# Sums on VectorE instead of GpSimd after the first weights are made, one sum of h made ahead, gates in fewer operations and asked for later

## The reference, cut to what matters

```python
def reference(x, itok_B_0_15, L0_cond_weights, L0_ffn_A, L0_ffn_B, L0_ffn_Wr):
    W = L0_cond_weights[itok_B_0_15]                 # (64, 64, 64), one 64x64 matrix per batch element
    y = jnp.einsum('bct,bcd->bdt', x, W)             # (64, 64, 1024)
    xf = y.reshape(-1, 1024)                         # 4096 tokens of 1024
    top_vals, top_idx = jax.lax.top_k(xf @ Wr.T, 16) # 64 experts, the best 16 of them
    gates = jax.nn.softmax(top_vals, axis=-1)
    G = zeros(4096, 64).at[rows, top_idx].set(gates)
    h = jnp.einsum('nd,krd->nkr', xf, A)             # 64 experts x rank 16 = 1024
    out = jnp.einsum('nkr,kdr->nd', h * G[:, :, None], B)
    return x + (out * 2.0).reshape(x.shape)          # everything in float32
```

## Time and profile before

| | |
|---|---|
| median of 3 runs | 787.85 us (786.58 to 791.64) |
| the profiled execution | 786.6 us, its span 784.5 us |
| TensorE (PE) matmuls | 733.8 us busy, 94% of the span, x3440 |
| TensorE weight loads (PEld) | 610.6 us, 78% |
| VectorE (DVE) | 451.1 us, 58%, x857 |
| ScalarE (ACT) | 277.0 us, 35% |
| GpSimd (POOL) | 230.6 us, 29%, x158 |
| mean granted TensorE clock | 0.971 |

### The profile page before, as it was taken

One profiled execution on the slowest core, in us unless ns is written; L12 is line 12 of the kernel. 1 busy time (PEld: TensorE's weight loads), 2 busy tenths in 40 slices (PEclk: granted clock), 3 DMA queues, 4 the chain that ended last, 5 costly groups with the idle time before them and its releaser, 6 DMA issues.

```text
span 784.5 us, 9378 instructions
## 1 busy us (share of the span) xinstructions
PE 733.8 (94%) x3440; PEld 610.6 (78%) x3440; DVE 451.1 (58%) x857; ACT 277.0 (35%) x526; POOL 230.6 (29%) x158
## 2 busy tenths in 40 slices
PE   6996969789999998999999989899999989899998
PEld 6784858578878786888888877788888878687886
DVE  1568689997532547784344266776444264768543
ACT  3545665346433443212222343212223244321310
POOL 1177720690002250084002124048000226009200
PEclk8998989989999999999999999999999999999999
DMA  9837337645796674646757675457667757454664
GB/s 320 326 138 266 160 123 285 250 193 209 256 374 226 220 267 167 250 184 215 258 213 265 229 281 208 170 187 245 236 239 270 264 221 268 141 196 146 241 211 164
DMA packets 57294, 178.15 MB, mean 227 GB/s; under 512 B 10914, under 2 KB 11042, under 8 KB 56738
## 3 DMA queue, kind: packets, MB, share of 16 engines
q1 hardware_dynamic: 55234, 173.04, 60.5%
q10 hardware_dynamic: 2016, 4.52, 1.6%
HBM read 131.40 MB, written 46.14 MB: 226 GB/s over the span
## 4 chain that ended last, share of the span: by engine, by line
PE 75%; DVE 18%; ACT 3%; DMA 2%; issue 1%; SPq 0%; DVEq 0%
PE Pb L263 34%; PE Pb L245 29%; PE Cb L225 7%; DVE Op L178 5%; PE S L279 4%; DVE Cq L358 3%; DVE Ox L178 1%; DVE Wt L196 1%; DMA xc<-in_x 1%; ACT Ex L313 1%; ACT Cq L369 1%; DVE G L339 1%; DVE s L326 1%; DVE Q L358 1%; DMA wbd<-in_wts 1%
## 5 line engine op out<-in xcount | busy, mean ns | idle before, releaser
L245 PE MATMUL Pb<-Op,Wt 128*128 128x512 f32 x1008 | 243.0, 396 | 6.6 <-DVE Op L178 6.5
L245 PEld LDWEIGHTS Pb<-Op,Wt 128*128 128x128 f32 x1008 | 190.5, 191 | 48.3 <-DVE Op L178 7.0
L263 PE MATMUL Pb<-Wt,Op 128*128 128x512 f32 x912 | 215.2, 394 | 8.6 <-DVE Op L178 8.6
L263 PEld LDWEIGHTS Pb<-Wt,Op 128*128 128x128 f32 x912 | 171.5, 190 | 45.3 <-DVE Op L178 9.2
L358 POOL TENSOR_TENSOR R<-R 128x512 f32<-128x512 f32 x64 | 93.0, 1478 | 318.5 <-DVE Op L178 258.0
L358 DVE TENSOR_TENSOR Q<-Pb,Q 128x512 f32<-128x512 f32 x112 | 77.1, 689 | 102.7 <-PE Pb L263 102.4
L178 DVE TENSOR_TENSOR Op<-R,Op 128x512 fp32r<-128x512 f32 x98 | 80.3, 845 | 62.7 <-ACT Op L176 62.7
L263 PE MATMUL Pb<-Wt,Ox 128*128 128x512 f32 x432 | 100.8, 391 | 0.0
L231 ACT COPY R<-Cb 128x512 f32<-128x512 f32 x64 | 37.5, 586 | 159.4 <-PE Cb L225 159.4
L263 PEld LDWEIGHTS Pb<-Wt,Ox 128*128 128x128 f32 x432 | 80.5, 188 | 16.3
L358 DVE TENSOR_TENSOR Cq<-Pb,Cq 128x512 f32<-128x512 f32 x64 | 44.1, 689 | 71.3 <-ACT Cq L369 42.3
(11 more groups left out here) (74 smaller groups left out, 518.4 us busy)
## 6 DMA issues: line engine op xcount, KB each, us to landing
Wt<-Wd SPq DMA_DIRECT2D x168, 512.0 KB, 4.7
Wd<-Wt SPq DMA_DIRECT2D x56, 512.0 KB, 2.9
Q<-in_x SPq DMA_DIRECT2D x32, 512.0 KB, 4.6
xc<-in_x SPq DMA_DIRECT2D x24, 512.0 KB, 4.2
out<-Q SPq DMA_DIRECT2D x32, 256.0 KB, 2.5
out<-Q SPq DMA_DIRECT2D x16, 512.0 KB, 3.4
BR<-in_x SPq DMA_DIRECT2D x12, 256.0 KB, 7.5
BR<-in_B SPq DMA_DIRECT2D x3, 1024.0 KB, 5.5
```

Source lines behind the costliest of these rows:

```text
L245: t = pe.run(lambda e, c=c, o=o, a=a, z=z: e.matmul(Pb[:, b, :], Wt[:, k, a, 128 * c:128 * c + 128], part(o, z), start=fresh and (c, a, z) ...
L263: t = pe.run(lambda e, c=c, o=o, k=k, a=a, z=z: e.matmul(Pb[:, b, :], part(o, a)[:, 128 * i:128 * i + 128], Wt[:, k, z, :], start=fresh an ...
```

## The change

- T1 is made on VectorE in all slabs, T2, T3 and T4 on VectorE in slabs 1 to 3 and on GpSimd in slab 0.
- The sums of h. Before, on GpSimd in one chain for each block: S1 = G21 + G22, S3 = G21 - G11, S2 = S1 - G11 at m = 0 of the second product, S4 at m = 1. Now D = G22 - G11 is made on VectorE at the last product of the first (m = 6), S2 = G21 + D at m = 0, S3 at m = 1, S1 = G11 + S2 at m = 2, S4 at m = 3, all on VectorE. S1 and S2 change places: S2 now lies in `u` or `xc`.
- In slab 0 two sums of B's quarters (T2b, T4b) go from VectorE to GpSimd. ScalarE's copies of weights into PSUM (`bank`) are dropped for B: VectorE subtracts from the source in SBUF.
- `top_c`: one operation over all four groups in place of four, with a sum of its own behind it, and the gates in two operations in place of four.
- `g_turn` is issued two steps later in the first half of the tokens and one step later in the second. In slabs 1 to 3 the second half's scores, their transposes, `top_a`, `top_b` and `top_c` stand one step earlier, with the splits that they need. The first score of a slab is issued one step later.
- The matmuls for slab 1's y stand at other steps of slab 0's second product (`SPREAD`), and their loads start earlier.

The same code in short, of the diff:

```diff
+SPREAD = [18, 19, 21, 22, 23, 25, 26, 27]
...
-            for i in range(4):
-                t = ve.run(lambda e, i=i: e.scalar_tensor_tensor(
-                    out=Ex[:, i, :], in0=s4[:, i, :], scalar=SENT, in1=Ex[:, i, :], op0=ALU.is_equal, op1=ALU.mult,
-                    accum_out=den[:, i:i + 1]), i == 3)
+            t = ve.run(lambda e: e.scalar_tensor_tensor(out=Ex[:, :, :], in0=s4[:, :, :], scalar=SENT, in1=Ex[:, :, :],
+                                                        op0=ALU.is_equal, op1=ALU.mult))
+            ve.after(t)
+            t = ve.run(lambda e: e.tensor_reduce(den[:, :], Ex[:, :, :], AXIS.X, ALU.add))
...
-            for i in range(4):
-                t = ve.run(lambda e, i=i: e.tensor_scalar(
-                    G[:, i, :, :], Ex[:, i:i + 1, :].to_broadcast([128, 2, 64]), den[:, i:i + 1], 2.0, ALU.mult,
-                    ALU.mult), i == 3)
+            for a in range(2):
+                t = ve.run(lambda e, a=a: e.scalar_tensor_tensor(
+                    out=G[:, :, a, :], in0=Ex[:, :, :], scalar=2.0,
+                    in1=den[:, :].rearrange("p (i k) -> p i k", k=1).to_broadcast([128, 4, 64]),
+                    op0=ALU.mult, op1=ALU.mult), a == 1)
...
-                t1[c] = add(gp, y11[c], y12[c], y11[c], split["y11"][c][1], R_ready[1][0], op=ALU.subtract)
+                t1[c] = add(ve, y11[c], y12[c], y11[c], split["y11"][c][1], R_ready[1][0], op=ALU.subtract)
...
-                t2[c] = add(gp, y11[c], y22[c], y11[c], split["T1"][c][1], R_ready[1][1], op=ALU.subtract)
+                t2[c] = add(ve if s else gp, y11[c], y22[c], y11[c], split["T1"][c][1], R_ready[1][1], op=ALU.subtract)
...
-                            raw["B21", j] = unit(28 + j, u[:, j, :], B_ready[3], free=(s_free, t_free)[j % 2],
-                                                 bank=(S[:, :], Tf)[j % 2])
+                            raw["B21", j] = unit(28 + j, u[:, j, :], B_ready[3])
...
+                        raw["D", j] = add(ve, s2_place(j), Cq[:, 1, j, :], Cq[:, 3, j, :], Cq_ready[1][j], Cq_ready[3][j],
+                                          u_busy[j] if s else op_free[NO + 4 + j // 2], op=ALU.subtract)
+
-                    if (m, j) in ((1, 2), (3, 3)):
+                    if (m, j) in ((1, 2), (3, 3 if s == 0 else 2)):
                         state["exps"] = top_a(state["t"])
-                    if (m, j) in ((1, 3), (4, 0)):
+                    if (m, j) in ((1, 3), (4, 0) if s == 0 else (3, 3)):
                         state["b"] = top_b()
-                    if (m, j) in ((2, 0), (4, 1)):
+                    if (m, j) in ((2, 0), (4, 1) if s == 0 else (4, 0)):
                         state["c"] = top_c(state["b"], state["exps"])
...
-                    if (m, j) == (0, 0):
+                    if (m, j) == (0, 1):
                         pe.after(wr_ready)
                         score(split["y21"], 1, True, False)
...
-                    if (m, j) == (2, 1):
+                    if (m, j) == (2, 3):
                         g_turn(state["c"], 0)
...
-                    if (m, j) == (4, 2):
+                    if (m, j) == (4, 3):
                         g_turn(state["c"], 1)
...
                         if m == 0:
-                            raw["T2b", c] = add(ve, B11, B11, B12, t, raw["T3b", c])
+                            raw["T2b", c] = add(gp, B11, B11, B12, t, raw["T3b", c])
                         elif m == 1:
-                            raw["T4b", c] = add(ve, u[:, c, :], u[:, c, :], B11, raw["B21", c], raw["T2b", c],
+                            raw["T4b", c] = add(gp, u[:, c, :], u[:, c, :], B11, raw["B21", c], raw["T2b", c],
                                                 op=ALU.subtract)
...
-                        raw["S1g", c] = add(gp, s1_place(c), q[0], q[1], Cq_ready[0][c], Cq_ready[1][c],
-                                            u_busy[c] if s else xc_free[c // 2])
-                        Cq_ready[0][c] = add(gp, q[0], q[3], q[0], Cq_ready[3][c], raw["S1g", c], op=ALU.subtract)
-                        Cq_ready[3][c] = add(gp, q[3], s1_place(c), q[3], Cq_ready[0][c], split["G11"][c][1],
-                                             op=ALU.subtract)
-                    elif m == 1:
-                        need("S2", c)
-                        Cq_ready[2][c] = add(gp, q[2], q[2], q[3], Cq_ready[3][c], split["G12"][c][1],
-                                             op=ALU.subtract)
+                        raw["S2g", c] = add(ve, s2_place(c), q[0], s2_place(c), Cq_ready[0][c], raw["D", c])
                     elif m < 6:
                         need(uses[m + 1], c)
...
+                        if m == 1:
+                            Cq_ready[0][c] = add(ve, q[0], q[3], q[0], Cq_ready[3][c], raw["S2g", c], op=ALU.subtract)
+                        elif m == 2:
+                            Cq_ready[3][c] = add(ve, q[3], q[3], s2_place(c), split["G11"][c][1], split["S2"][c][1],
+                                                 Cq_ready[0][c])
+                        elif m == 3:
+                            (u_busy if s else S2_split)[c] = Cq_ready[2][c] = add(
+                                ve, q[2], q[2], s2_place(c), split["G12"][c][1], Cq_ready[3][c], op=ALU.subtract)
...
-                    if more and (step >= 20 if s == 0 else step in range(2, 24, 3)):
-                        k = step - 20 if s == 0 else step // 3
+                    if more and (step in SPREAD if s == 0 else step in range(2, 24, 3)):
+                        k = SPREAD.index(step) if s == 0 else step // 3
```

More of the change, by code:

```diff
@@ L10 @@
 ALU = mybir.AluOpType
+AXIS = mybir.AxisListType
 ACT = mybir.ActivationFunctionType
@@ L147, in adaln_ffn @@
         x0 = [raws[i // 2][:, 2 * (i % 2):2 * (i % 2) + 2, :].rearrange("p a b -> p (a b)") for i in range(8)]
-        Tf = T[:, :, :].rearrange("p a n -> p (a n)")
-        S1_split = [None] * 4
-        S1x = [xc[:, c // 2, 512 * (c % 2):512 * (c % 2) + 512] for c in range(4)]
+        S2_split = [None] * 4
+        S2x = [xc[:, c // 2, 512 * (c % 2):512 * (c % 2) + 512] for c in range(4)]
         bank_free, bank_n = [None] * 4, [0]
@@ L516, in sum_t1, with s2_place @@
             def sum_t1(c):
-                t1[c] = add(gp, y11[c], y12[c], y11[c], split["y11"][c][1], R_ready[1][0], op=ALU.subtract)
+                t1[c] = add(ve, y11[c], y12[c], y11[c], split["y11"][c][1], R_ready[1][0], op=ALU.subtract)
             def sum_t2(c):
-                t2[c] = add(gp, y11[c], y22[c], y11[c], split["T1"][c][1], R_ready[1][1], op=ALU.subtract)
+                t2[c] = add(ve if s else gp, y11[c], y22[c], y11[c], split["T1"][c][1], R_ready[1][1], op=ALU.subtract)
             def sum_t3(c):
-                t3[c] = add(gp, y12[c], y22[c], y12[c], split["y12"][c][1], R_ready[1][1], op=ALU.subtract)
+                t3[c] = add(ve if s else gp, y12[c], y22[c], y12[c], split["y12"][c][1], R_ready[1][1], op=ALU.subtract)
             def sum_t4(c):
-                t4[c] = add(gp, y21[c], y21[c], y11[c], split["y21"][c][1], t2[c], op=ALU.subtract)
-            def s1_place(c):
-                return u[:, c, :] if s else S1x[c]
+                t4[c] = add(ve if s else gp, y21[c], y21[c], y11[c], split["y21"][c][1], t2[c], op=ALU.subtract)
+            def s2_place(c):
+                return u[:, c, :] if s else S2x[c]
             def need(name, c):
@@ L601, in adaln_ffn @@
                             need("y22", c)
+                        if s:
+                            for c in late[j]:
+                                need("y12", c)
                         sum_t2(j)
                     elif m == 3:
-                        for c in ((0, 1, 2, 3), (), (), ())[j]:
-                            need("y12", c)
-                        for c in late[j]:
+                        if s == 0 and j == 0:
+                            for c in range(4):
+                                need("y12", c)
+                        for c in (late if s == 0 else early)[j]:
                             need("T2", c)
@@ L698, in adaln_ffn @@
                     elif m < 6:
                         need(uses[m + 1], c)
-                        if m == 4:
-                            (u_busy if s else S1_split)[c] = split["S1"][c][1]
+                        if m == 1:
[6 more added lines that the diff above has]
+                                ve, q[2], q[2], s2_place(c), split["G12"][c][1], Cq_ready[3][c], op=ALU.subtract)
@@ L702, in adaln_ffn @@
                     elif more:
                         split.setdefault("next", []).append(operand(y21[c], R_ready[0][1]))
-                    if s == 0 and step in (18, 20):
-                        xc_free[(step - 18) // 2] = S1_split[step - 17]
-                        load_x(1, (step - 18) // 2)
+                    if s == 0 and step in (14, 16):
+                        xc_free[(step - 14) // 2] = S2_split[step - 13]
+                        load_x(1, (step - 14) // 2)
```

(4 more changed lines are left out.)

13 lines of the change are left out of this document (5 added, 8 removed).

## The result

| | before | after |
|---|---|---|
| median of the runs made together | 787.62 us (4 runs, 786.58 to 791.64) | 747.17 us (4 runs, 744.97 to 747.66) |
| the profiled execution, its span | 786.6, 784.5 us | 745.0, 743.2 us |
| mean granted TensorE clock | 0.971 | 0.991 |

The ratio is 0.947, with a 95% interval of 0.944 to 0.950. The forecast was 751; the profiled executions differ by 41.6 us where the sum said 36.9.

What follows compares the result with a forecast made beforehand. TensorE's matmuls are busy 94% of the span, so only its idle or lower-clock time can be gained. -24.7 - 13.4 + 1.2 = -36.9 us from 786.6 gives 749.7; the median lies 1.25 above: 751 us, range 742 to 764.

Steps and rivals of the forecast that it cites:

- Slabs 1 to 3: Both waits for gates, the lower clock behind them and a 0.7 us split wait go: -24.7 us.
- Gates in fewer operations: The new `top_c` takes about 1.8 us against 1.7 before and gains nothing: 0, between -0.3 and +0.3 a time.
- Slab 0, first product: Sum of the router weights, T1 with first gates, and second gates: -13.4 us, bounds -6 and -16.
- (a): Slab 0, first product: the score that waited 1.3 us for the router weights stands a step later, -1.3 us.
- (b): Slab 0, first product: T1 on VectorE, P5 waits about 1.0 us, first gates ready before asked for: -9.2 us.
- (c): Slab 0, second gates: the 6.29 us wait shrinks by one step, -2.7, and -0.2 for transposes starting sooner; lower clock stays.
- Slab 0, second product: VectorE sets the pace; last split 0.9 us later, 1.3 for the clock, x loads 1.0 less: together +1.2 us.
- the load of x: Slab 0, second product: loads start four steps earlier, shortening the 1.9 us wait by 1.0, bounds 0 and 1.9.
- B: Rival: the gates' wait in slabs 1 to 3 is smaller but not gone, +12 us, 763 us; chance 0.12.
- C: Rival: VectorE becomes the bound, operations with two SBUF inputs costing 1.00 us, 801 us; chance 0.03.
- A: Rival: GpSimd holds VectorE more than counted in slab 0, +6 us, 757 us; chance 0.15.
- D: Better case: slab 0's second product loses 5 us less and the clock stays up, below 743 us; chance 0.04.

Runs made afterwards that it cites:

- e1: The kernel before with only the gates' transposes later, two steps in the first half of the tokens and one in the second, all slabs: 760.53 us.
- e2: The changed kernel with the transposes of the gates back at their old two places: 763.83 us.
- e3: The changed kernel with the sums of y and h back on GpSimd in slabs 1 to 3: 745.03 us.
- e7: The changed kernel with the old form of `top_c`, eight small operations and the reciprocal: 745.99 us.
- e8: The changed kernel with the sum D made at m = 0 of the second product, in front of S2, instead of at m = 6: 748.77 us.
- e11: The changed kernel with all sums of y and of B in slab 0 on VectorE: 745.93 us.
- e5: The changed kernel with slab 0's T2b, T4b and T1b moved from GpSimd to VectorE: 745.00 us.
- e6: The changed kernel with ScalarE's copies of B's blocks into PSUM kept, as before the change: 745.76 us.
- e9: The changed kernel with slab 0's second transposes of gates one more step later and the gating behind them in pairs: 746.53 us.

## Why the prediction was right, term by term

The large term, slabs 1 to 3, was right in its mechanism and within 1.5 us. The terms of slab 0 were off by 1.8 us one way and 4.6 us the other, and it is their size, small beside the whole, that kept the forecast near.

**Slabs 1 to 3: -24.7 predicted, -26.2 measured.** Slab 1 gave 7.3 us (183.34 to 176.00), slab 2 8.9, slab 3 the rest. The mechanism is shown by e1 (27 us from two constants, part of them in slab 0) and e2. The chain of VectorE up to the second gates was counted at 10.0 us against 16.3 available, room 6; it takes 11.8 (273.38, where the transposes of the scores end, to 285.15), and the room is 4.4. That the sums on VectorE cost nothing holds, and e3 adds what the prediction left open: no gain by them is seen either. So the step "VectorE gets new work into the room" was right, and brought nothing.

**Gates in fewer operations: 0 predicted, no difference seen** (e7). The new form takes 1.95 us, and the old one took 1.78, which the prediction read as 1.7.

**Slab 0, first product: -13.4 predicted, -11.6 measured** (Q2 starts at 126.16, before at 137.80).

| | predicted | measured |
|---|---|---|
| (a) the router weights | -1.3 | -1.8, start of the step behind 33.27 to 31.48 |
| (b) T1 and first gates | -9.2 | -8.8, start of P3 80.80 to 70.22 less (a) |
| (c) second gates | -2.9 | -1.1: at the start of step (5, 0) it is -3.3 (116.03 to 102.14, less (a) and (b)), with the low clock of before in it, and 2.2 go to the low clock behind it |
| sum | -13.4 | -11.6 |

In (a) the wait of 1.3 us is gone, and the other 0.5 is not the edit's: P2 starts 0.8 us later, and its first 12 matmuls take 3.70 us (19.74 to 23.44) where 4.85 went before. Other executions with the same program up to there differ as much: in e7 P2 starts at 19.31 and those 12 take 4.8.

In (b), P5 waits 1.25 where "about 1.0" was said. Its last two T1 splits take 1.29 together, 3.44 in the earlier trace rows:

```profile
42.32 4.69 DVE L360 TENSOR_TENSOR R<-R 128x512 f32<-128x512 f32 x4
...
59.47 1.29 DVE L179 TENSOR_TENSOR Op<-R,Op 128x512 fp32r<-128x512 f32 x2
```

The T1 sums cost 4.69, not 4 x 0.60, as GpSimd's sums of A run until 45.3 instead of 43; there VectorE had the time. In (c) the wait fell by one step as said, 6.29 to 3.71. "The low clock behind it stays" is the step that was off: it did not stay the same. The windows of TensorE in the change (stretch, length, busy, clock, DMA share, GB/s), from step (5, 0) on:

```profile
102.14:107.09 4.95, 4.95 (x14) 0.54 0.57 211
```

12 matmuls take 4.95 us at a mean granted clock of 0.54, so mostly at 1.2 GHz, 2.2 more than at full clock; before, the 12 behind the longer wait took 3.95 (112.08 to 116.03), 1.2 more. The difference, 1.0 us, is over half of what (c) missed.

**Slab 0, second product: +1.2 predicted, -3.4 measured** (103.65 to 100.22 us). This is the term that failed, in its sign. It had three parts. First, the chain. The chain of VectorE ("TensorE gets its last split 0.9 us later than now") came 1.5 earlier: Q6 is entered 33.22 us after Q2's start, 34.69 before. The steps of m = 0 were 4.1 as counted, with T4b in the last as said. The steps of m = 1 were put at 4.6, both of GpSimd's sums at full price, and took 4.0, 3.5 the first; the end behind them took 1.8 where 2.3 was said. Together the chain is 2.9 shorter than counted, less 0.6 for a start that was 1.7 late and not 1.1. The prediction had its own sentence for this ("if GpSimd's sums fall beside drains more often, it is 5 us less"), and took the other side. Second, the low clock of 1.3 in front of Q6 did not come: 123 matmuls behind the 2.68 us wait take 28.19, which is full clock. That is luck more than merit: behind 3.01 us in e8 and 2.77 us in e11 the same 123 take 29.79 and 29.78. Third, the load of x: 1.0 was booked and all 1.9 went. That the earlier loads did it is argued and not shown, as no kernel takes `SPREAD` back; what speaks for it is that e1, with the old places, waits 3.3 us for x, and that e5, e6 and e9, with the new ones, wait 0.4, 1.1 and 0.2. The sign that the prediction gave for this stretch, a wait of some 5 us before Q6 and a smaller one in Q1, did not come either: it is 2.68 before Q6, and 1.27 and 3.11 in Q1.

**The rivals.** B and C are out: no wait and no late step in slabs 1 to 3. A had GpSimd holding VectorE more than counted; the opposite held, and what decided is the instruction that lies beside GpSimd's sum. D, the better case, named both things that came (less lost in the second product, the clock staying up), and the result lies between it and the forecast's centre.

**A rule weighed in the prediction.** The blocked split at 129.81 ends 0.55 us behind the end of GpSimd's sum, the blocked `BR<-BR` of the earlier trace rows 0.54, the half-blocked `Wt` operation at 149.55 0.54. So in these three the blocked operation has the last 0.54 us to do when GpSimd is done, and 0.14 of its 0.68 has passed. The Trainium skill's page "SBUF — State Buffer", section "Who interferes with whom", has the two contend for an exclusive lock, and its summary says that the second to issue "fully blocks" until the first finishes; by that, each would end 0.68 behind. The trace agrees with the lock and not with the last 0.14.

## What to carry to other kernels

When the busiest engine waits for a side chain, first ask later for its result, and count the room of the chain in steps of that engine; here two constants alone brought 27 of 40 us, and moving 36 sums a slab to another engine showed no gain (e3). Where an in-order queue feeds the busy engine, name what stands behind the thing that you stop waiting for: its lateness is the next wait. A GpSimd sum beside a VectorE operation with two SBUF inputs costs VectorE more (1.1 us) than making the sum itself (0.6), but beside a drain from PSUM it costs nothing (0.68 at 148.95), so price it by what lies beside it.
